# Mamba block on one core: step projection, skip products and convolution placed elsewhere in TensorE's order

## The reference

```python
x = hidden_states
xn = layernorm(x)
x = x + mamba(xn) + ffn(xn)

def mamba_dir(xz, conv_w, conv_b, xproj_w, dtproj_w, dt_bias, A_log, Dp):
    x, z = xz[:, :256], xz[:, 256:]
    u = silu(causal_conv(x, conv_w) + conv_b)            # 4 taps per channel
    x_dbl = einsum('bdl,kd->bkl', u, xproj_w)            # 8 + 16 + 16 rows
    delta = softplus(einsum('dr,brl->bdl', dtproj_w, x_dbl[:, :8]) + dt_bias)
    Bm, Cm = x_dbl[:, 8:24], x_dbl[:, 24:40]
    dA = exp(delta * A)                                  # 16 states
    h = scan(dA, delta * Bm * u)                         # along the sequence
    y = einsum('bdln,bnl->bdl', h, Cm) + Dp * u
    return y * silu(z)
# mamba: forward + reversed backward direction, then out_proj
# ffn: Hadamard transform, 4-bit activations, ternary weights
```

## Time and profile before

| | us |
|---|---|
| median of three runs | 977.38 |
| lowest, highest | 975.98, 980.18 |
| the profiled execution | 976.08 |
| its span | 974.0 |
| mean granted TensorE clock | 0.864 of full speed |
| DVE, ACT, PE, POOL busy | 800.2, 782.1, 765.9, 750.2 |
| DMA queue, share of 16 engines | 31.6% |

### The profile page before, as it was taken

The page is one execution under the profiler, slowest core; times in us unless marked ns, Lnnn a source line. Parts: engine busy times, 40 slices in busy tenths (PEclk is TensorE's granted clock), DMA queues, the critical chain, the costliest instruction groups (busy, mean ns, idle before and its releaser), DMA issues.

```text
span 974.0 us, 13835 instructions
## 1 busy us (share of the span) xinstructions
PE 765.9 (79%) x3873; PEld 384.4 (39%) x3873; DVE 800.2 (82%) x838; ACT 782.1 (80%) x1454; POOL 750.2 (77%) x454
## 2 busy tenths in 40 slices
PE   3486977689786977979689697878978697797994
PEld 1233443343433435334353344434443343433452
DVE  2278988898788878888888887889878887897995
ACT  2599995899878987789967998589986898878970
POOL 2159887788768977789787887878886798777994
PEclk9788988889787988979889797988978798897797
DMA  3424225070620607024070512507052070702400
GB/s 91 113 66 118 48 79 107 4 163 4 141 55 30 135 3 172 24 70 91 30 166 3 126 38 70 124 3 162 3 126 68 10 154 3 172 14 68 95 7 27
DMA packets 51433, 72.53 MB, mean 74 GB/s; under 512 B 6704, under 2 KB 19920, under 8 KB 51408
## 3 DMA queue, kind: packets, MB, share of 16 engines
q1 hardware_dynamic: 50976, 71.97, 31.6%
q10 hardware_dynamic: 432, 0.26, 0.1%
HBM read 60.68 MB, written 11.53 MB: 74 GB/s over the span
## 4 chain that ended last, share of the span: by engine, by line
POOL 29%; issue 27%; PE 18%; ACT 15%; DVE 8%; DMA 2%; POOLq 1%; SPq 0%; DVEq 0%; ACTq 0%
POOL hst L678 22%; PE pb L792 5%; DVE hst L569 5%; ACT da L416 4%; POOL dbx_t L688 4%; PE b_ps L879 4%; ACT dbx_t L405 2%; PE y L894 2%; PE b_ps L864 1%; PE y L891 1%; POOL t_log L694 1%; ACT xn L308 1%; PE pb L856 1%; DVE b_ps L557 1%; PE pb L811 1%
## 5 line engine op out<-in xcount | busy, mean ns | idle before, releaser
L678 POOL TENSOR_TENSOR hst<-hst,c_rep 128x1024 f32<-128x1024 f32 x256 | 600.6, 2365 | 170.8 <-DVE hst L569 170.1
L569 DVE TENSOR_TENSOR_SCAN hst<-da,b_ps 128x512 f32<-128x512 f32 x512 | 586.3, 1202 | 43.1 <-ACT da L416 21.4
L879 PE MATMUL b_ps<-ident,dbx_t 128*128 128x128 f32 x1536 | 246.6, 301 | 158.3 <-DVE hst L569 157.4
L416 ACT ACTIVATE da<-rep,neg_a 128x511 f32<-128x511 f32 x512 | 336.2, 710 | 5.8 <-DVE hst L569 3.8
L879 PEld LDWEIGHTS b_ps<-ident,dbx_t 128*128 128x128 f32 x1536 | 181.0, 151 | 281.2 <-DVE hst L569 255.7
L405 ACT ACTIVATE dbx_t<-du_t,b_t 128x256 f32<-128x256 f32 x576 | 247.0, 496 | 2.5 <-PE b_ps L879 1.7
L894 PE MATMUL y<-hst,sum_sel 128*32 128x512 f32 x1024 | 148.9, 657 | 3.0 <-POOL hst L678 3.0
L792 PE MATMUL pb<-xnt,conv_wt 128*128 128x512 f32 x256 | 121.0, 617 | 0.8 <-ACT xnt L316 0.8
L688 POOL TENSOR_TENSOR dbx_t<-du_t,b_t 128x1024 f32<-128x1024 f32 x48 | 91.3, 1903 | 2.7 <-ACT du_t L388 2.7
L864 PE MATMUL b_ps<-t_log,spread_sel 32*128 32x512 f32 x256 | 73.4, 679 | 14.3 <-POOL t_log L740 9.8
L557 DVE TENSOR_TENSOR b_ps<-b_ps,b_rep 128x1024 f32<-128x1024 f32 x64 | 78.0, 1219 | 5.4 <-PE b_ps L864 5.4
(11 more groups left out here) (111 smaller groups left out, 588.5 us busy)
## 6 DMA issues: line engine op xcount, KB each, us to landing
rep<-d_scr SPq DMA_DIRECT2D x128, 256.0 KB, 9.1
c_rep<-bc_scr SPq DMA_DIRECT2D x64, 256.0 KB, 4.8
d_scr<-t_pos SPq DMA_DIRECT2D x15, 512.0 KB, 3.0
b_rep<-bc_scr SPq DMA_DIRECT2D x64, 64.0 KB, 2.2
x_ln<-x SPq DMA_DIRECT2D x8, 256.0 KB, 3.3
x_res<-x SPq DMA_DIRECT2D x8, 256.0 KB, 2.8
out<-x_res SPq DMA_DIRECT2D x8, 256.0 KB, 7.1
conv_wt<-conv_w SPq DMA_DIRECT2D x2, 512.0 KB, 5.8
```

Of the source, the lines that this page charges most:

```text
L416: nc.scalar.activation(da[s % 2][:, j, 1:L], rep[d][h][:, j, 1:L], ACT.Exp, scale=neg_a[:, d, h, j, q:q + 1]).then_inc(decay_done, 1)
L569: nc.vector.tensor_tensor_scan(hst[s % RING][:, j, :], da[s % 2][:, j, :], b_ps[:, j, :], 0.0, ALU.mult, ALU.add).then_inc(scan_done, 1)
L678: nc.gpsimd.tensor_tensor(hst[s % RING][:, two, :], hst[s % RING][:, two, :], c_rep[d][:, q:q + 1, :].broadcast_to([P, 2, L]), ALU.mult).t ...
L879: ins = tr(b_ps[:, j, P * c:P * (c + 1)], dbx_t[(NX * d + q - 1) % 2][:, c, NJ * h + j, :, :].rearrange("p r e -> p (r e)"), ident[:, :])
```

## The change

Five things, all for the preparation of the next unit or the place of a job in a list:

1. `steps(e, 1)` goes from behind the second half of slot 1's inputs to ahead of it, right behind `b_transposed`. `steps(e, 0)` stays.
2. x_dbl stands once: `xproj` has 64 columns, its product and its copy 64 rows, and both step products read partitions 0 to 63. In the start four weight loads fall away and the clears get smaller.
3. ACT's `keep_bt` goes from behind the second decays and the last inputs of slot 2 to ahead of them.
4. The skip products leave `sum_states` and stand in slot 3 ahead of the second half of the inputs.
5. The lumps of `conv` go half a slot forward: the first (half 0) from the middle of slot 7 to the end of slot 6, the second (half 1) from the end of slot 7 to the middle.

```diff
-        xproj = [sb(f"xproj{d}", [P, NH, 2, XC]) for d in range(2)]
+        xproj = [sb(f"xproj{d}", [P, NH, XC]) for d in range(2)]
...
-                for h in range(NH):
-                    sp.dma_start(xproj[d][:, :, h, 0:DR + 2 * NS], xproj_t[d]).then_inc(w_loaded, DMA)
-                    sp.dma_start(dtw[d][XC * h:XC * h + DR, :], dt_t[d]).then_inc(w_loaded, DMA)
+                sp.dma_start(xproj[d][:, :, 0:DR + 2 * NS], xproj_t[d]).then_inc(w_loaded, DMA)
+                sp.dma_start(dtw[d][0:DR, :], dt_t[d]).then_inc(w_loaded, DMA)
...
-                nc.scalar.activation(xdbl[d][:, :], pb[:, 1, :], ACT.Copy).then_inc(xdbl_ready, 1)
+                nc.scalar.activation(xdbl[d][0:XC, :], pb[0:XC, 1, :], ACT.Copy).then_inc(xdbl_ready, 1)
...
                         inputs_t(d, U, 2, 2)
+                        if nxt:
+                            keep_bt(e, V)
...
                         inputs_t(d, U, 2, 3)
                         if nxt:
-                            keep_bt(e, V)
                             softplus_in(e, V)
...
-                mm(pb[:, h, :], dtw[d][XC * h:XC * (h + 1), P * h:P * (h + 1)], xdbl[d][XC * h:XC * (h + 1), :], start=True, stop=True).then_inc(dt_filled, 1)
+                mm(pb[:, h, :], dtw[d][0:XC, P * h:P * (h + 1)], xdbl[d][0:XC, :], start=True, stop=True).then_inc(dt_filled, 1)
...
+            def skip_products(b, d):
+                step = slice(None, None, -1 if d else 1)
+                pe.wait_ge(u_ready, 2 * (2 * b + d) + 2)
+                for h in range(NH):
+                    mm(y[:, h, :], skip[:, d, h, :], u[d][:, h, step], start=False, stop=False, skip_group_check=True)
...
-                if s == SKIP_AT - 1:
-                    pe.wait_ge(u_ready, 2 * (2 * b + d) + 2)
-                    for n in range(NH):
-                        mm(y[:, n, :], skip[:, d, n, :], u[d][:, n, step], start=False, stop=False, skip_group_check=True)
...
+                        steps(e, 1, xdbl_ready, V + 1)
+                    if s == SKIP_AT:
+                        skip_products(b, d)
...
                     if s == 7 and not last(b):
-                        if d == 0:
-                            pe.wait_ge(xnt_ready, b + 2)
-                        conv(d, U + 2, 0, range(TAPS), dut_ready, 2 * V + 1)
+                        conv(d, U + 2, 1, range(TAPS), dut_ready, 2 * V + 2)
                     next_inputs(s, 1)
...
                     if s == 1 and nxt:
-                        steps(e, 1, xdbl_ready, V + 1)
                         steps(e, 0, bt_ready, V + 1)
...
-                    if s == 7 and not last(b):
-                        conv(d, U + 2, 1, range(TAPS), dut_ready, 2 * V + 2)
+                    if s == 6 and not last(b):
+                        if d == 0:
+                            pe.wait_ge(xnt_ready, b + 2)
+                        conv(d, U + 2, 0, range(TAPS), dut_ready, 2 * V + 1)
```

More of the change, by code:

```diff
@@ L282, in _ @@
             sp.wait_ge(out_stored, DMA * NB)
-        W_LOADS = 7 + 8
+        W_LOADS = 7 + 4
         WIN = hst[0][:, 0, 0:DI]
@@ L798, in x_proj @@
                 for h in range(NH):
-                    ins = mm(pb[:, 1, :], xproj[d][:, h, :, :].rearrange("p r c -> p (r c)"), u[d][:, h, :], start=h == 0, stop=h == NH - 1)
+                    ins = mm(pb[0:XC, 1, :], xproj[d][:, h, :], u[d][:, h, :], start=h == 0, stop=h == NH - 1)
                 ins.then_inc(xdbl_filled, 1)
```

## The result

The changed kernel takes 997.26 us (median of 4 runs, 994.09 to 999.81) against 978.26 us for the kernel before beside it: a ratio of 1.019, with a 95% interval from 1.016 to 1.023. It is slower. The forecast was 986.5 us with a range of 972 to 996: the side was right, the forecast loss of 9 us was half of the 19 that came, and the median lies just outside the range.

The account below looks back on a forecast made before the run. No engine is full, so waits between engines bound the kernel. Convolution's 25.6 us loss less step product and start gains gave -2.5 us at full clock, +14.7 at low; mixed, 977.4 + 9 = 986.5 us, range 972 to 996.

Parts of the forecast that it names:

- What bounds the kernel, and the cut: No engine is full, so engines' waits bound it; each unit is cut at the second make_u and first log1p.
- Convolution: First lump at the end of slot 6 delays make_u: 1.85 us lost forward to backward, 1.8 backward to forward, 7 times each.
- Skip products: Moved into PE's 5.65 us idle time in slot 3: nothing gained in forward units, 0.9 us won in backward ones.
- The rival in which the skip products were the path: Backward unit's end hangs on PE, not POOL: all 3.6 us won in each of 7 units, 967.5 us; chance 0.14.
- Step product: Make_u to log1p: full clock wins 2.35 us forward, 1.6 backward on average; low clock at x_proj leaves 1.3 and 0.2.
- Two products at once: Step products overlapped on separate partition halves, 1.13 us together; now apart on one half, taken as 1.0 us each.
- Start: Fewer DMA issues and clears, covered by the first convolution: nothing; the first unit wins 0.4 us.
- Sum: Whole kernel: -2.5 us at full clock, +14.7 at low clock everywhere at x_proj; low in two of three units, +9.
- The clock that holds: Rival: PE keeps full clock at x_proj, 975 us, no difference that can be told; chance 0.23.
- Moves hidden: Rival: the moves are hidden anyway, time stays 977.4 us; chance 0.04.
- The full slow convolution: Rival: backward unit's first lump wholly at low clock, 7.3 us instead of 3.63, x_proj always slow; 1001 to 1011 us; chance 0.14.
- the signs: New DVE wait 3 to 4.5 us, no wait for u, ACT's second wait under 0.7, log1p to make_u 37.5 and 42.7 us.

Follow-up runs that it names:

- e2: The kernel before with only the two convolution lumps moved half a slot forward; 1014.9 us, ratio 1.038.
- e3: The kernel before with only the skip products moved into slot 3; 978.1 us over 10 runs, ratio 1.000.
- e1: The changed kernel with both convolution lumps back in slot 7, their old place; 964.8 us, ratio to the kernel before 0.988.
- e4: The kernel before with only the earlier first step product, the single x_dbl and the earlier b_t copy; 961.7 us, ratio 0.982.
- e5: The changed kernel with the skip products back at the end of slot 3; 994.1 us, ratio 1.019.
- e10: e4 with B transposed copied at its old place, behind the second decays and inputs of slot 2; 956.4 us, ratio 0.979.
- e12: e4 with x_dbl stored twice, as in the kernel before; 958.0 us, ratio 0.982.
- e8: The changed kernel with both lumps in the middle of slot 7, behind the first copies and ahead of the second; 990.6 us, ratio 1.016.
- e6: The changed kernel with the first copies for slot 1 done three times over, to keep PE busy ahead of x_proj; 985.6 us, ratio 1.010.
- e11: e4 with the second step product ahead of the transposes too; 943.8 us, ratio 0.967.

## Why the prediction was right in direction and wrong in size

*What bounds the kernel, and the cut.* The cut served: it shows in which stretch each edit acts. But the edits did not stay in their stretches. The lumps cost 1.44 us in the forward stretch behind make_u too (e2), and the skip products up to 1.5 us in a stretch where they were put at nothing (e3).

*Convolution.* Right. Forward to backward 1.85 us were forecast; e2 measured 1.94, and 37.3 us stand in every unit whose clock holds. Backward to forward 1.8 were forecast and 1.29 came. The first lump begins 27.5 us after log1p, where 27.6 was forecast, and the chain behind it was 14.16 for 14.2. The 0.9 us added for the low clock came in three of seven units only: there the first lump took 4.7 to 4.9 us and the stretch 42.7 to 42.9; in the other four the clock had risen again before the lump (3.67 us in the rows above), and the stretch was 41.5 to 41.8. By the lumps alone the kernel loses 38 us, and 31 to 33 when set beside the other edits.

*Skip products.* The failed step. They were put at 0.9 us won in each of 7 backward units and nothing lost in the forward ones. Three pairs of kernels differ in them alone. Moving them changed the time by 0.0% in the kernel before (e3), cost 3 us by the medians when added to the steps (e1 against e4; 6 by the ratios), and 3 by the medians, nothing by the ratios, in the changed kernel (against e5): nothing to 6 us lost, no part of it clear of the noise, where 6.3 were to be won. "In the forward unit nothing is gained" was right, and that nothing would be lost was taken with it. The idle time in front of slot 3's inputs, 5.65 us and now 3.93 in a unit of e3 and 2.21 in one of the changed kernel, appears again two slots later, in smaller pieces, ahead of the PE work that leads to the lumps, and brings the low clock there: 39.4 to 39.6 us in three units and 38.2 in one. The mean of the forward stretch is 0.87 us above what the lumps alone were forecast to make it (38.35 against 37.48), 6 us in all (e5 takes that away, e3 shows it by itself).

In the backward unit the quantization began where the forecast had it: POOL's scale step ended 20.15 us after log1p (at 492.27) and the first quantization step started at 20.18, where 20.1 was forecast (after, timelines of POOL and DVE):

```profile
512.18 0.24 POOL L727 TENSOR_SCALAR qscale<-amax 128x4 f32<-128x4 f32 x1
512.45 0.18 DVE L518 RECIPROCAL qinv<-qscale 128x4 f32<-128x4 f32 x1 [1.50 <-POOL qscale L727]
```

But the gain of 0.9 us was read off one of the later units (21.03). The mean of the seven before is 20.76, so the skip products alone could win 0.57 (20.19 in e3), and in the changed kernel they win 0.24, since with them back it is 20.42 (e5); the steps alone bring it to 20.20 (e4). The forecast time of that step came out right, then, and in the changed kernel mostly not by the move that was given the credit. The rival in which the skip products were the path falls: in the changed kernel the residual (L580) is added from 508.02 on, and POOL's scale step is done more than 3 us behind that.

*Step product.* A second term that was too kind. With x_proj at the higher clock the gain was put at 2.35 us forward and 1.1 or 2.5 backward, and it came: 18.11 us against 20.53 and 20.78 in the same units before, 16.92 and 16.93 against 19.47 and 18.07 (2.5 and 1.1 won, both as forecast), and a forward mean of 18.18 with the filler. At the low clock 1.3 and 0.2 us were to be left. The three forward units with a slow x_proj took 20.74 to 20.91 us, against 20.52 to 20.79 before: nothing was left. The four backward ones took 18.56 to 20.22, 0.2 us more than before on average. In the three forward units two things add up that the forecast had at 0.25 us and at nothing: DVE's 1.35 us wait for the last sum, and the second step product at the low clock (2.07 us, and ACT waited up to 1.64 us for it, where the forecast's sign was under 0.7). That x_proj was slow in 7 of 14 units and not in two of three went the other way. The means came to 1.19 us forward and 0.53 backward, where the mixture was 1.65 and 0.67: 4 us less in all. The b_t copy was costed at nothing and may cost some (e10).

*Two products at once.* Measured at the start, where both stand together in both kernels: 1.98 us in the changed kernel, 1.13 in the one before, at a granted clock of 1.00 in both. The loss of overlap is real there. In mid-run it did not decide (e12).

*Start.* "Nothing" and a gain of 0.4 us were forecast, and in the profile of the changed kernel the first log1p is 2.8 us later. Most of this is chance and no effect of the change. The first make_u is at 62.25 us here and at 60.14 and 60.47 in e5 and e8, which have the same start, against 60.54 in the kernel before and 62.09 in e2, which has the start of the kernel before. The difference is mostly the clock at the first x_proj: 3.38 us here and 3.60 in e2, 1.90 in e5 and e8. The first unit's stretch is 18.72 us here, 18.61 in e5 and 17.23 in e8, against 17.64 before; in e8 the forecast 0.4 was won. What the change itself costs is 0.85 us for the pair of step products, and that does not show in the first make_u of e5 and e8.

*Sum.* From profile to profile: forecast +9; +6 (skip products), +4 (steps), +3 (start, mostly chance), -3.6 (backward boundary) and -0.7 (last piece) give the 18 us between the two profiles. So the +9 had two errors on one side, skip products and steps, and the backward boundary on the other took back a part by luck. *Rivals.* The clock that holds (975 us) would have needed more than a clock that holds at x_proj: e6 has that and takes 985.6. "Moves hidden" is far off. The full slow convolution did not come: the longest first lump in the changed kernel took 4.91 us, not 7.3. Of the signs, the new DVE wait (3.17 us and up to 4.4) and no wait for u in mid-run came as said; log1p to make_u was 38.35 and 42.15 us where 37.5 and 42.7 were named.

## What to carry to other kernels

Ahead of moving a job in an engine's order, ask which short jobs behind it are read first by the next engine on the path, and how much long work now stands ahead of the last of them: a wait that appears at the first of them can be harmless (3.2 us here, e8), while two lumps ahead of the second copies, with the low clock at x_proj that came with them, cost 31 to 38 us. Filling one hole can open another: follow the engine's idle time to where it comes out again and look at the clock there. And where half a pair is moved ahead of a wait, look whether the other half can go too: that alone brought 14 to 18 us (e11 against e4). A gain read off one unit is not the mean of seven, and gains of two moves that act on the same wait do not add.

## What the runs showed of the hardware

In e3 PE's clock fell to the lower level after pieces of idle time that were each under 2 us (1.75, 0.46 and 1.09 us), and one batch on, with 1.46 in place of 1.75, it didn't. What followed took about double: eight passes of the sum 1.93 us for 1.06, eight transposes 1.96 for 1.09. The cost of an idle stretch is thus not its own length only but also the doubling of what follows, if that is on the path.

Extra work that computes the same twice more ended that at x_proj: it took 1.93 us in all 14 units with the filler, where 7 of 14 took 2.91 to 3.68 without it, and the kernel was 10 to 12 us faster (e6). The clock also differs between profiles of kernels with the same code at that place: the first x_proj took 3.38 us in the changed kernel and 1.90 in e5 and e8.

Two fp32 products of 64 rows and 512 columns took 1.13 us together when they read different halves of the partitions, and 1.98 us when they read the same half (before and after, start of the program, granted clock 1.00).
